# Attention probabilities times values in 32-column stationary blocks, in a fused cross-attention and mixture-of-experts kernel

## The reference

```python
qh = (q @ w_q + b_q)...; kh = (k @ w_k + b_k)...; vh = (v @ w_v + b_v)...   # 16 heads of 16
scores = jnp.einsum('bhqd,bhkd->bhqk', qh, kh) * D_HEAD ** (-0.5)
attn = jax.nn.softmax(jnp.where(mask == 0, -10000.0, scores), axis=-1)
out = jnp.einsum('bhqk,bhkd->bhqd', attn, vh)            # 77 keys per head
x = x + tanh(g_xattn[0]) * (out... @ w_o + b_o)
x = x + tanh(g_ffn[0]) * (top-2 experts of 4, and a shared expert)(layernorm(x))
```

## Time and profile before

| | |
|---|---|
| median of three runs | 1040.31 us (1035.69 to 1040.54) |
| the profiled execution's own time | 1040.25 us |
| its span, first to last instruction | 1038.5 us |
| TensorE matmuls busy | 959.3 us, 92% of the span |
| ScalarE busy | 499.8 us, 48% |
| VectorE busy | 553.3 us, 53% |
| mean granted clock | 0.961 |

### The profile page before, as it was taken

How to read it: one execution, slowest core, us unless ns; L and a number is a source line. 1 busy time by engine, 2 the same in 40 slices (tenths; PEclk the granted TensorE clock), 3 DMA queues, 4 the chain that set the end, 5 groups by cost and what they waited for, 6 DMA issues and landing times.

```text
span 1038.5 us, 21453 instructions
## 1 busy us (share of the span) xinstructions
PE 959.3 (92%) x6299; PEld 855.3 (82%) x6300; DVE 553.3 (53%) x1253; ACT 499.8 (48%) x1804; POOL 466.5 (45%) x639
## 2 busy tenths in 40 slices
PE   6778999999999998898898799999999999999995
PEld 4556778788887888888788699999999999999995
DVE  4564566766657524867876444444444444444442
ACT  3787797988889753333234322222222222222221
POOL 4345454646546323325573144444444444444442
PEclk9597999999999998898999999999999999999998
DMA  5212422221321121221124122222222222222221
GB/s 162 68 35 80 119 66 66 65 77 52 94 65 42 62 71 52 78 86 57 63 79 130 49 40 40 40 40 40 40 40 40 36 40 40 37 39 40 40 40 21
DMA packets 56862, 61.70 MB, mean 59 GB/s; under 512 B 15642, under 2 KB 45183, under 8 KB 56799
## 3 DMA queue, kind: packets, MB, share of 16 engines
q1 hardware_dynamic: 42871, 43.15, 13.4%
q0 software_dynamic: 12864, 17.57, 10.5%
q10 hardware_dynamic: 1064, 0.21, 0.1%
HBM read 34.78 MB, written 25.82 MB: 58 GB/s over the span
## 4 chain that ended last, share of the span: by engine, by line
PE 74%; ACT 11%; DVE 6%; issue 5%; POOL 2%; DMA 1%; ACTq 0%; DVEq 0%; SPq 0%; POOLq 0%
PE p_s L308 24%; PE p_t L318 12%; PE p_f L1781 7%; PE p_m L1729 6%; PE p_f L1796 6%; ACT prob L1038 5%; PE p_f L332 4%; PE p_m L1685 3%; PE p_t L1716 2%; PE p_t L322 2%; ACT xn L1012 1%; PE p_m L293 1%; PE p_s L1704 1%; PE p_m L1739 1%; PE p_m L1758 1%
## 5 line engine op out<-in xcount | busy, mean ns | idle before, releaser
L199 POOL DMA_INDIRECT out_rows<-yout,add_at x67 | 107.2, 1599 | 196.1 <-DVE yout L263 196.1
L1038 ACT ACTIVATE prob<-p_s,negmax 128x77 f32<-128x77 f32 x512 | 160.7, 358 | 9.0 <-DVE negmax L1307 8.5
L270 DVE TENSOR_TENSOR hid<-p_s,sil 128x688 f32<-128x688 f32 x67 | 58.6, 875 | 164.2 <-ACT sil L237 125.8
L237 ACT ACTIVATE sil<-p_s 128x688 f32<-128x688 f32 x67 | 50.0, 746 | 192.9 <-PE p_s L308 192.9
L1781 PE MATMUL p_f<-xnT_hi,swgu_hi 128*128 128x256 f32 x352 | 111.1, 316 | 16.3 <-DVE shid L1328 11.5
L1038 ACT ACTIVATION_READ_ACCUMULATOR prob<-p_s,negmax 128x1 f32 x512 | 122.4, 240 | 0.0
L308 PE MATMUL p_s<-wgu_hi,fxT_hi 128*128 x402 | 110.9, 383 | 2.7 <-DVE hid L258 2.7
L816 POOL TENSOR_TENSOR prob<-prob,rinv 128x616 f32<-128x616 f32 x64 | 78.2, 1224 | 63.5 <-DVE rinv L1314 63.3
L308 PE MATMUL p_s<-wgu_lo,fxT_hi 128*128 x402 | 105.1, 370 | 0.0
L308 PE MATMUL p_s<-wgu_hi,fxT_lo 128*128 x402 | 104.5, 369 | 0.0
L1781 PE MATMUL p_f<-xnT_lo,swgu_hi 128*128 128x256 f32 x352 | 103.0, 293 | 0.0
(11 more groups left out here) (224 smaller groups left out, 2450.3 us busy)
## 6 DMA issues: line engine op xcount, KB each, us to landing
xr<-in_x SPq DMA_DIRECT2D x16, 256.0 KB, 2.9
x_scratch<-xr SPq DMA_DIRECT2D x16, 256.0 KB, 2.0
xn_scratch<-xn SPq DMA_DIRECT2D x16, 256.0 KB, 2.1
xt_scratch<-xnT SPq DMA_DIRECT2D x16, 256.0 KB, 2.0
xin<-xt_scratch SPq DMA_DIRECT2D x16, 256.0 KB, 3.4
x1in<-x_scratch SPq DMA_DIRECT2D x16, 256.0 KB, 3.1
out_rows<-syout SPq DMA_DIRECT2D x16, 256.0 KB, 2.3
raw<-in_L_ffn_ed SPq DMA_DIRECT2D x4, 688.0 KB, 4.2
```

Of the source, the lines that this page charges most:

```text
L199: pool.indirect_dma_start(out, bass.IndirectOffsetOnAxis(add_at[k][:, :], 0), yout[k][:, :], None, compute_op=ALU.add).then_inc(s_add, 16)
L270: nc.vector.tensor_tensor(hid[:, 0:FF], p_gu[:, FF:2 * FF], sil[:, :], ALU.mult).then_inc(s_hid, 1)
L1038: last = act.activation(prob[n % 2][t][:, m * PW + h * SK:m * PW + (h + 1) * SK], p_s[:, 2 * t + h // 4, col:col + SK], ACT.Exp, bias=negm ...
```

## The change

The ten 128-column matmuls of a unit become sixteen with 32 columns. Two heads together (a pair) have 154 rows of (head, key) and always lie in two neighbouring chunks; the stationary operand of a pair and a chunk is 32 columns wide, 16 for each head. The four pairs of a half take the four column groups of the array (`tile_position=(0, d0)` with `d0` 0, 32, 64 and 96) and write partitions `d0` to `d0+31` of the same bank. Each reads its own chunk of `pT`. The order is half, then first or second chunk of the pair, then pair. `vblk` shrinks from 2 x 10 x 128 to 2 x 16 x 32 columns; its DMAs are as many and as large as before, with other targets, and the `memset` covers less.

```diff
+def pair_chunk(pair):
+    return pair * 2 * SK // P
...
-                yield m, hh, k, k + n, m * CH + row // P, row % P
+                yield m, hh, k, k + n, row // P, row % P
...
-        vblk = sb("vblk", [P, 2, KC * CH, P])
+        vblk = sb("vblk", [P, 2, KC * HH, 2 * DH])
...
-                    sp.dma_start(vblk[r0:r0 + k1 - k0, b % 2, c, hh * DH:(hh + 1) * DH],
+                    pair = hh // 2
+                    at = (m * (HH // 2) + pair) * 2 + c - pair_chunk(pair)
+                    sp.dma_start(vblk[r0:r0 + k1 - k0, b % 2, at, hh % 2 * DH:(hh % 2 + 1) * DH],
...
-                for c in range(KC * CH):
-                    m = c // CH
-                    last = nc.tensor.matmul(p_m[:, m * UT * P:(m + 1) * UT * P], vblk[:, b % 2, c, :], pT[:, c, :],
-                                            start=(c % CH == 0), stop=(c % CH == CH - 1))
+                for m in range(KC):
+                    for k in range(2):
+                        for pair in range(HH // 2):
+                            d0 = pair * 2 * DH
+                            last = nc.tensor.matmul(p_m[d0:d0 + 2 * DH, m * UT * P:(m + 1) * UT * P],
+                                                    vblk[:, b % 2, (m * (HH // 2) + pair) * 2 + k, :],
+                                                    pT[:, m * CH + pair_chunk(pair) + k, :],
+                                                    start=(k == 0), stop=(k == 1), tile_position=(0, d0))
                 last.then_inc(s_PV, 1)
```

## The result

The changed kernel took 1010.42 us (median of 4 runs, 1009.03 to 1012.42), the kernel before 1039.19 (4 runs, 1035.69 to 1040.54): a ratio of 0.973, 95% interval 0.9709 to 0.9751. That is 28.8 us less, where 10.5 were forecast and the range ended at 1022. The sign was right and the size was not.

A forecast was written before the change was run, and what follows sets the result against it. TensorE was taken as the bound, ScalarE not far behind. Eight late-load units −5.8, six others −3.2, units 1 and 2 −2.1, unit 14 +0.2 make −10.9 us, cut to −10.5: 1040.3 to 1030 us, range 1022 to 1058.

The forecast's parts named there:

- Every product is on the chain, and what it gains passes on as far as ScalarE follows: All 16 units: the product is on TensorE's chain, so its gain reaches the end if ScalarE can follow.
- A slot is 0.216 us for 32 columns as for 128; alone it would be 32 slots: Product: a slot is the distance of neighbouring matmul records, 0.216 us; without overlap 32 slots replace 20.
- Column groups run together as row groups do: Product: matmuls on different column groups run at once at full speed, assumed from the row groups of the scores.
- The rival of the uncovered loads: Product: loads don't pass waiting matmuls of other groups; 0.033 us at each of 15 group changes gives 1038 us; chance 0.19.
- The failed step: Product: a matmul's second record waits a slot, at most two groups work, so 17 slots for 20, −0.65 us per unit.
- More than 4 of 16 failed overlaps eat the gain: Product: the no-overlap rival decides once more than 4 of 16 possible overlaps fail; its full case 1084 us, chance 0.15.
- The layout change costs 0.12 us in the odd-numbered units: Ahead of the product in six units: going from 128 to 32 columns costs 0.10 us and a load, together 0.12.
- ScalarE takes 1.18 us in even steps: Unit 12: ScalarE's idle time lets it take up to 1.18 us before it becomes the bound, more than the 0.73.
- The GpSimd and DMA edits cost nothing: The smaller `memset` saves about 1.3 us but GpSimd then waits anyway; the value DMAs are covered: nothing.
- the rival of four groups: Product: all four groups at once, first records passing waiting second ones, 8 slots, −29 us, 1011 us; chance 0.05.
- The clock stays at 1.00 from 105 us: Stage from 105 us on: the granted clock should stay at 1.00, as it did before the change.
- the forecast's clock rival: Stage from 105 to 398 us: mean clock falls to 0.93 because TensorE does less, 1051 us; chance 0.06.

The follow-up runs named there:

- e2: The changed kernel with all sixteen matmuls in column group 0, three quarters of the output left out: 1077.65 us, 1.0383 of the kernel before.
- e1: The changed kernel with the two chunks of a pair made neighbours, four records in a row per column group: 1013.78 us, 0.9746 of the kernel before.
- e8: The changed kernel with three matmuls of each pair in turn, then each pair's fourth, six records in a row per group: 1024.62 us (one execution).
- e5: The changed kernel with the pair as outermost loop, eight records in a row per column group: 1037.73 us, 1.0004 of the kernel before.
- e10: The changed kernel with GpSimd's key blocks ahead of its `rstd1` instead of behind: 1006.36 us, 0.9716 of the kernel before.
- e3: The changed kernel with 64-column blocks in two column groups, twelve matmuls per product: 1015.61 us, 0.9787 of the kernel before.
- e4: The changed kernel with only the first chunk of each pair, eight matmuls for sixteen, the rest left out: 1010.2 us, 0.973 of the kernel before.

## Why the prediction was wrong in its size

- **Every product is on the chain, and what it gains passes on as far as ScalarE follows.** Right for ScalarE, but GpSimd had to follow too (below). e2 shows it upward: 12 slots are 2.59 us, and its steps are 23.19 and 26.29 us against 20.59 and 23.70 before. Odd steps show it downward.
- **A slot is 0.216 us for 32 columns as for 128; alone it would be 32 slots.** Right: 32 slots in e2.
- **Column groups run together as row groups do.** Right, and loads to another group pass waiting matmuls: seven loads had started 0.04 us into the product. The rival of the uncovered loads (0.19) fell. The Trainium skill (TensorE: Matmul & The Clock Gate, Part 3, The mechanism) has a load overlap matmuls in flight only where the row group differs; here all groups use all 128 rows, and the trace disagrees.
- **The failed step: "The two records of one matmul are neighbours and need the same group, so the second waits a slot for the first... Never are more than two groups at work", hence 17 slots.** The second record waits, but the next matmuls pass it. It is 8 slots. The prediction called matmuls out of order unlikely because "in no row does a matmul start ahead of an earlier one"; no row of before has a part of the array free while a matmul for another part waits ahead, so this was no evidence. The Trainium skill (the same page and section) states that matmuls start and end strictly in program order; e1, e8 and e5 show starts out of it, past up to three waiting records. Beyond three, e8 and e5 show just the holding up that the prediction assumed.
- **More than 4 of 16 failed overlaps eat the gain.** A miscount: 17 slots for 32 records are 15 overlaps, and three failures eat it. No term of the sum hangs on it.
- **The layout change costs 0.12 us in the odd-numbered units.** The last matmul of `down` starts 0.12 us after the one before it, and the product 0.21 us after that: 0.09 us. Right, and it was no matter.
- **ScalarE takes 1.18 us in even steps.** This bound did not bite in the forecast (0.73) but did in the outcome, and it was nearly right: units 6, 10 and 12 kept 1.37 of 2.66 us.
- **The GpSimd and DMA edits cost nothing.** No wait for `s_vblk` appeared, and e5, which has these edits, takes the time of the kernel before. But neither the forecast nor the rival of four groups saw GpSimd's key blocks: they made the steps after units 4 and 8 longer by 1.37 and 0.08 us, although the product was 2.66 shorter. e10 returned 4.9 us of steps.
- **The clock stays at 1.00 from 105 us.** Wrong in part: stretches of 3.4 us at 0.50 stand at 117.7, 145.0 and 346.4 us, and the step of unit 14 is 0.96 us longer than before, with the last of them in it. They are not the forecast's clock rival (mean 0.93); from 105 to 375 us the mean is 0.98.

The rival of four groups at once gave 1011 and the kernel took 1010.4. Its mechanism held, but so close a hit is in part luck. By the profiled spans the kernels are 31.3 us apart. Units 5, 7, 9, 11, 13 and 15 gave 15.3 us (12.8 from the five steps from unit 5 on, 2.5 from unit 15's product), where that rival had 15. For the other ten it had some 14 and they gave 11.0: units 0 to 3 9.3 and units 6, 10 and 12 4.1, while the steps of units 4, 8 and 14 took back 2.4. The last 4.9 us lie behind unit 15's product, where nothing was changed and nothing was forecast; there the chip granted the half clock for 25.9 us instead of 39.3. That is one execution of each, and whether the change causes it stays open.

## What to carry to other kernels

Where each row of a stationary operand is mostly zeros, narrower blocks in several column groups pay, since records of different groups share a slot: here 20 slots became 8. Write them so that the groups alternate, since the same sixteen matmuls give everything (1010 us) or nothing (1038 us) by the order of three loops. And when an engine that leads by little becomes faster, look at once at what the next engine does in each kind of step: part of the gain of the even steps stayed with ScalarE, taking a copy off ScalarE brought out a wait for GpSimd in two of three of them, and the two steps with key blocks gained nothing through an ordering on GpSimd that had cost some 0.5 us each before.

## What the runs showed of the hardware

- Up to four fp32 matmuls on four column groups start within 0.04 us, each with its own load; 32 records took 1.86 us in four groups, 24 took 2.74 in two, 32 took 7.03 in one.
- TensorE starts matmuls out of program order across column groups, past three waiting records of each other group and not past a fourth (second group at slot 0, 2 and 4 with 4, 6 and 8 records in a row).
- The shorter the product, the more of its stage ran at half clock: the mean from 105 to 375 us is 1.00 with 20 slots a product, 0.99 with 14 to 15 (e8), 0.98 with 12 (e3) and with 8, and 0.95 with 4 (e4). That the one causes the other was not tried apart.
